# Quantisation without GpSimd and a new division of labour in the routing stage of a two-layer attention kernel

## The chip, the cores and the metric

One Trainium2 chip, one core. The metric is the device time in microseconds (us) of one execution, the median of several.

## The reference

What is computed, with B, S, D = 8, 512, 256, 16 heads and 8 experts:

```python
x = x + tanh(g_xattn[0]) * L0_xattn(layernorm(x), ctx)       # softmax attention
x = x + tanh(g_ffn[0])   * L0_ffn(layernorm(x))              # 2 of 8 experts per token, then a layer norm
x = x + tanh(g_xattn[1]) * L1_xattn(layernorm(x), ctx)
x = x + tanh(g_ffn[1])   * L1_ffn(layernorm(x))

def fake_quant_fp8(t):                                       # in L1_ffn, for x and for weight
    scale = 448.0 / maximum(max(abs(t)), 1e-12)
    return (t * scale).astype(float8_e4m3fn).astype(float32) / scale
L1_ffn = einsum('bsd,od->bso', fake_quant_fp8(x), fake_quant_fp8(weight)) + bias
```

The maximum is over the whole tensor, so nothing of the last layer can be scaled before the last layer norm is done.

## The kernel before

The kernel runs as ten stages, one after the other (`build`): `setup`, `project`, attention 0, `route`, `place`, `experts`, `combine`, attention 1, `merge`, `quantise`. Each stage has a program for each engine; a stage begins on all engines once the one before it has ended on all. Within a stage the order on each engine is written out by hand, and semaphores tie the engines together. Activations stand in SBUF as 128 partitions x 4 tiles x 256 columns for each of the 8 batches (`S.X` the residual, `S.BIG` the work copy), so an operation on a batch is 128x1024.

`route` (L979) ends attention 0. For each batch b, the reciprocals of the softmax sums are spread over the rows with two matmuls for each half k (`spread`, L671 and L672, all into the one PSUM bank pD); ScalarE copies the half to SBUF (`take_spread`, L1043); GpSimd multiplies the batch with it (`scale`, L1082); TensorE makes the output product (L975); VectorE adds it to the residual (L1100), takes the statistics (L341, L345), GpSimd raises to -1/2 (`Norm.power`, L350 and L353), VectorE normalises (`Norm.apply`, L361), TensorE turns the batch (L957), ScalarE takes it out (L1049), TensorE makes the router's logits (L964), VectorE copies them (L1107), the last thing in its round. VectorE clears a tile of zeros first (L1093), from which SyncE stores 8 MB. The reciprocal of the two last batches (`division.invert(LATE)`, L650) and its rounding into two parts (`cut_high`, `cut_low`) come at the stage's start.

`merge` (L1832) is the same for attention 1, with spreading banks for both halves, the scaling already on VectorE (L1897) and the normalising on ScalarE (L1876) with a product and a shift that GpSimd makes (L1887, L1889). VectorE also takes each batch's greatest magnitude (L1911). The reciprocal of the last two batches (L650) stands in VectorE's third round, `cut_low` (L659) in the fourth.

`quantise` (L1931) takes the maximum over partitions with GpSimd's all-reduce (L1971); VectorE makes scale, its inverse and the bias row from it, one after the other (L2035 to L2049). Then per batch: ScalarE scales (v, L1986); VectorE masks the exponent (m, L1821); GpSimd makes m into a rounding constant (max, then multiply, L1825); VectorE adds and subtracts it (L2076, L2079), the result in bf16; TensorE turns it (L2014); ScalarE takes it out (L2000, one buffer); TensorE multiplies with the quantised weight, four tiles of two bf16 matmuls (L2024) and one f32 matmul of a row of ones with the bias row (L2025); VectorE scales and adds the residual (L2062); SyncE stores. On TensorE each batch is turned, then waits for ScalarE's copy, then multiplied.

## Time and profile before

| | |
|---|---|
| Median of 3 runs | 1856.8 us (1854.93 to 1860.06) |
| The profiled execution | 1859.13 us, span 1857.1 us |
| Busy: TensorE, VectorE, ScalarE, GpSimd | 85%, 69%, 52%, 38% of the span |
| `route` | 519.4 to 605.8 us |
| `merge` | 1704.2 to 1760.8 us |
| `quantise` | 1761.1 us to the end |

The span holds instructions from first to last; about 2 us of the execution lie around it. Busy shares are averages over stages with different limits: what a change in one stage is worth is read from that stage's own timeline. In timeline rows the first number is the start and the second the duration; "x2" merges two instructions, and the bracket at the end gives how long the engine had been idle and who released it.

### The profile page before, as it was taken

The numbers are of one execution on the slowest core, as the hardware profiler recorded it, in microseconds if no ns is written. First come the engines' busy times: TensorE is split into PE (matmuls) and PEld (weight loads), VectorE is DVE, ScalarE is ACT, GpSimd is POOL, SyncE is SP. The second block draws the span as 40 slices with busy tenths as digits, with TensorE's granted clock in tenths as the row PEclk, the third lists the DMA queues.
The fourth block names the chain that finished last, engine by engine and source line by source line (L and its number), as shares of the span: only waits on it lengthen the run. The fifth ranks groups of instructions, "written<-read, shape, count | busy, mean of one in ns | idle before, by whom it ended". The sixth has DMA issues, their size and how long they took to land. (4 is left out here: it accounts for less than half of the span.)

```text
span 1857.1 us, 30481 instructions
## 1 busy us (share of the span) xinstructions
PE 1581.8 (85%) x11963; PEld 1035.1 (56%) x11963; DVE 1289.3 (69%) x1990; ACT 958.1 (52%) x1291; POOL 708.4 (38%) x954
## 2 busy tenths in 40 slices
PE   4873999999978269999999999688479999998558
PEld 3761333333357259999999999445223333334423
DVE  3655999999764856655555553478489999996843
ACT  2550888888822033444444444245248888885321
POOL 1651555555232044533333333333124545540252
PEclk9995999999987579999999999899779999999855
DMA  6556455555351212122212211356554555541001
GB/s 205 199 215 109 107 120 124 118 125 122 75 234 59 68 57 81 47 87 92 91 48 90 89 46 41 112 210 225 135 87 120 122 124 116 127 120 39 0 27 64
DMA packets 116766, 198.71 MB, mean 107 GB/s; under 512 B 28480, under 2 KB 62080, under 8 KB 115600
## 3 DMA queue, kind: packets, MB, share of 16 engines
q1 hardware_dynamic: 82480, 110.20, 20.0%
q0 software_dynamic: 34144, 86.56, 18.3%
q8 instruction: 95, 1.56, 0.4%
q14 instruction: 47, 0.39, 0.1%
HBM read 117.77 MB, written 77.87 MB: 105 GB/s over the span
## 5 line engine op out<-in xcount | busy, mean ns | idle before, releaser
L902 DVE TENSOR_REDUCE a_nmax<-a_ring 128x2 f32<-128x1024 f32 x512 | 608.7, 1220 | 40.1 <-PE a_ring L814 39.6
L884 ACT ACTIVATE a_pexp<-a_ring 128x1024 f32<-128x1024 f32 x512 | 522.6, 1027 | 195.7 <-PE a_ring L824 195.7
L836 PE MATMUL a_pout<-a_pexp,values 128*17 128x256 f32 x4096 | 321.5, 387 | 0.7 <-ACT a_pexp L884 0.7
L814 PE MATMUL a_ring<-a_k,a_q 64*128 64x512 f32 x1024 | 243.5, 474 | 54.1 <-DMA a_q<-qs 43.8
L1523 ACT ACTIVATE e_full<-e_pH,b1T 128x256 f32<-128x256 f32 x320 | 133.8, 469 | 272.3 <-PE e_pH L1483 269.8
L824 PE MATMUL a_ring<-a_q,a_k 64*128 64x512 f32 x1024 | 258.8, 502 | 12.8 <-DMA a_q<-a_nT 9.3
L1552 DVE TENSOR_TENSOR e_hid_lo<-e_full,e_hid_hi 128x512 fp32r<-128x512 f32 x160 | 128.2, 805 | 159.5 <-ACT e_hid_hi L1531 158.8
L824 PEld LDWEIGHTS a_ring<-a_q,a_k 64*128 64x128 f32 x1024 | 96.6, 185 | 235.2 <-DVE a_nmax L902 134.1
L1502 PE MATMUL e_pY<-fc_w_hi,e_hid_hi 128*128 128x256 f32 x640 | 186.0, 291 | 9.7 <-DVE e_hid_lo L1552 9.7
L1483 PE MATMUL e_pH<-e_rowsT_hi,fc_w1T_hi 128*128 128x256 f32 x640 | 182.3, 285 | 1.5 <-DVE e_rowsT_lo L1398 1.5
L1483 PE MATMUL e_pH<-e_rowsT_lo,fc_w1T_hi 128*128 128x256 f32 x640 | 182.1, 285 | 0.0
L1483 PE MATMUL e_pH<-e_rowsT_hi,fc_w1T_lo 128*128 128x256 f32 x640 | 182.0, 284 | 0.0
L1502 PE MATMUL e_pY<-fc_w_hi,e_hid_lo 128*128 128x256 f32 x640 | 180.9, 283 | 0.0
L1502 PE MATMUL e_pY<-fc_w_lo,e_hid_hi 128*128 128x256 f32 x640 | 180.9, 283 | 0.0
L814 PEld LDWEIGHTS a_ring<-a_k,a_q 64*128 64x128 f32 x1024 | 99.8, 192 | 130.7 <-DMA a_q<-qs 45.1
L723 POOL DMA_DIRECT2D a_k<-key_centre x56 | 32.0, 572 | 334.7 <-PE a_ring L824 334.7
L836 PEld LDWEIGHTS a_pout<-a_pexp,values 128*17 128x17 f32 x4096 | 68.3, 95 | 129.5 <-issue 126.6
L1502 PEld LDWEIGHTS e_pY<-fc_w_hi,e_hid_hi 128*128 128x128 f32 x640 | 122.4, 191 | 12.9 <-DVE e_hid_lo L1552 12.3
L1483 PEld LDWEIGHTS e_pH<-e_rowsT_hi,fc_w1T_hi 128*128 128x128 f32 x640 | 123.9, 194 | 1.9 <-DVE e_rowsT_lo L1398 1.9
L1483 PEld LDWEIGHTS e_pH<-e_rowsT_lo,fc_w1T_hi 128*128 128x128 f32 x640 | 124.0, 194 | 0.0
L1483 PEld LDWEIGHTS e_pH<-e_rowsT_hi,fc_w1T_lo 128*128 128x128 f32 x640 | 123.9, 194 | 0.0
L1502 PEld LDWEIGHTS e_pY<-fc_w_lo,e_hid_hi 128*128 128x128 f32 x640 | 122.6, 192 | 0.0
(295 smaller groups left out, 2570.1 us busy)
## 6 DMA issues: line engine op xcount, KB each, us to landing
outs<-a_osb SPq DMA_DIRECT2D x64, 256.0 KB, 2.7
fc_raw<-in_L_ffn_fc_w SPq DMA_DIRECT2D x16, 1024.0 KB, 5.6
a_k<-ks POOLq DMA_DIRECT2D x112, 128.0 KB, 3.4
a_q<-qs POOLq DMA_DIRECT2D x112, 128.0 KB, 3.6
BIG<-outs SPq DMA_DIRECT2D x64, 128.0 KB
ytok<-r_zeros SPq DMA_DIRECT2D x8, 1024.0 KB, 10.2
c_yg<-ytok POOLq DMA_DIRECT2D x16, 512.0 KB, 7.7
a_k<-ks POOLq DMA_DIRECT2D x112, 64.0 KB, 3.5
```

What stands on the lines that cost most here:

```text
L723: e.dma_start(k[j][lo:hi, :, :].bitcast(F32), S.key_centre[l][:, at].rearrange("s (o t) -> s o t", o=1).broadcast_to([hi - lo, 2, SEQ])).t ...
L814: mm = e.matmul(max_bank(m)[:, hh, :], q[j][at, p, t * P:(t + 1) * P], k[j][at, p, :], start=True, stop=True)
L824: mm = e.matmul(score_bank(n * U + i)[:, hh, :], k[j][at, p, t * P:(t + 1) * P], q[j][at, p, :], start=True, stop=True)
L836: mm = e.matmul(pout[n % 2][32 * h:32 * h + VW, at], v[:, b * TPB + t, g * HG + h, :], pexp[t][:, h, at], start=(t == 0 and half == 0), st ...
L884: e.activation(pexp[t][:, 2 * p:2 * p + 2, :], score_bank(n * U + i)[:, :, :], ACT.Exp).then_inc(exped, 1)
L902: e.tensor_reduce(nmax[n % 2][:, :].rearrange("p (x y t) -> p x y t", x=2, y=2)[:, :, p, t], max_bank(m)[:, :, :], AX.X, ALU.max, negate=T ...
L1483: mm = e.matmul(pH[q][:, f % 2, :], w1T[x][pl][:, k, f * P:(f + 1) * P], rowsT[j][pr][:, k, :], start=(k == 0 and n_pass == 0), stop=(k == ...
L1502: mm = e.matmul(pY[:, t, :], hid[pl][:, f, t * P:(t + 1) * P], w2[x][pr][:, f, :], start=(f == 0 and n_pass == 0), stop=(f == KF - 1 and n ...
L1523: ins = e.activation(full[q % 2][:, f % 2, :], pH[q][:, f % 2, :], ACT.Silu, bias=S.b1T[:, ds(n * KF + f, 1)])
L1552: e.tensor_tensor(hid[LO][:, 2 * q:2 * q + 2, :], full[q % 2][:, :, :], hid[HI][:, 2 * q:2 * q + 2, :], ALU.subtract).then_inc(lo, 1)
```

## The change

In `quantise`, GpSimd does nothing per batch any more. The maxima of the partitions (128x1) are turned into a row on TensorE and reduced by VectorE; 448 over the maximum is computed on one element and widened to all partitions by a matmul with a row of ones. The rounding constant is made by ScalarE, as Relu(m*MAGIC - LEAST), and VectorE's two operations add LEAST back (now scalar_tensor_tensor with two tensors and a constant). The bias row becomes three bf16 rows, at partitions 0, 32 and 64 of a 96-row operand that GpSimd clears, and its matmul is bf16 with 96 rows of ones. v has three buffers in the place of two, the turned batch two in the place of one; the order on TensorE stays turn, wait, multiply.

In `route`, the spread half is multiplied straight out of PSUM by VectorE (no copy on ScalarE, no GpSimd multiply), and ScalarE normalises with GpSimd's shift. The clearing of the zeros moves to GpSimd. TensorE's orders around `output` shift by one place, and the reciprocal stands behind VectorE's first four scalings. In `merge` the last reciprocal moves in front of the first update, `cut_high` to ScalarE's start and `cut_low` behind the first statistics. The diff, cut:

```diff
--- before.py
+++ after.py
+    def power_and_shift(self, e, b):
+        j = b % 2
+        self.power(e, b, j)
+        e.wait_ge(self.powed, b + 1)
+        e.tensor_tensor(self.product[j][:, :], self.mv[j][:, :, 0], self.rstd[j][:, :], ALU.mult).then_inc(self.shifted, 1)
+        e.wait_ge(self.shifted, 2 * b + 1)
+        e.tensor_scalar(self.shift[j][:, :], self.product[j][:, :], -1.0, None, ALU.mult).then_inc(self.shifted, 1)
+
+    def activate(self, e, b, src, dst):
+        j = b % 2
+        e.wait_ge(self.shifted, 2 * b + 2)
+        for t in range(TPB):
+            e.activation(dst[:, t, :], src[:, t, :], ACT.Identity, bias=self.shift[j][:, t:t + 1],
+                         scale=self.rstd[j][:, t:t + 1]).then_inc(self.normed, 1)
...
+    def scale(self, e, src, b, k):
+        rows = self.S.BIG[:, b * TPB + k * KD:b * TPB + (k + 1) * KD, :].rearrange("p t d -> p (t d)")
+        e.wait_ge(self.spread, b * KD + k + 1)
+        e.tensor_tensor(rows, rows, src[:, :], ALU.mult).then_inc(self.scaled, 1)
...
-                        e.wait_ge(division.copied, b * KD + k)
+                        e.wait_ge(division.scaled, b * KD + k)
                     division.spread_rows(e, pD, b, k)
 
                 def output(b):
-                    e.wait_ge(division.scaled, b + 1)
+                    e.wait_ge(division.scaled, (b + 1) * KD)
...
                 output(0)
                 spread(2, 0)
+                output(1)
                 spread(2, 1)
-                output(1)
                 for b in range(B):
                     if b + 3 < B:
                         spread(b + 3, 0)
                     turn_normed(b)
+                    if b + 2 < B:
+                        output(b + 2)
                     if b + 3 < B:
                         spread(b + 3, 1)
-                    if b + 2 < B:
-                        output(b + 2)
                     logits(b)
...
-                def take_spread(b, k):
-                    e.wait_ge(division.spread, b * KD + k + 1)
-                    if b >= 2:
-                        e.wait_ge(division.scaled, b - 1)
-                    e.activation(wide[b % 2][:, k, :], pD[:, :], ACT.Copy).then_inc(division.copied, 1)
...
+                for b in range(-1, B):
+                    if b >= 0:
+                        take_turned(b)
+                    if b + 1 < B:
+                        nb.activate(e, b + 1, S.X[:, tiles(b + 1), :], S.BIG[:, tiles(b + 1), :])
...
-                def scale(b):
-                    e.wait_ge(division.copied, (b + 1) * KD)
-                    rows = S.BIG[:, tiles(b), :].rearrange("p (k t) d -> p k (t d)", k=KD)
-                    e.tensor_tensor(rows, rows, wide[b % 2][:, :, :], ALU.mult).then_inc(division.scaled, 1)
-                scale(0)
-                scale(1)
+                e.memset(zeros[:, :, :], 0.0).then_inc(zeroed, 1)
                 for b in range(B):
-                    nb.power(e, b, b % 2)
-                    if b + 2 < B:
-                        scale(b + 2)
+                    nb.power_and_shift(e, b)
...
-                e.memset(zeros[:, :, :], 0.0).then_inc(zeroed, 1)
+                for b in range(2):
+                    for k in range(KD):
+                        division.scale(e, pD, b, k)
                 division.invert(e, LATE)
-                division.cut_low(e, LATE)
                 for i in range(B + 2):
                     if i < B:
                         x = S.X[:, tiles(i), :]
                         e.wait_ge(yd, i + 1)
                         e.scalar_tensor_tensor(out=x, in0=pY[i % 2][:, :, :], scalar=S.tg[:, 0:1], in1=x,
                                                op0=ALU.mult, op1=ALU.add).then_inc(upd, 1)
+                        if i and i + 1 < B:
+                            division.scale(e, pD, i + 1, 1)
                         e.wait_ge(upd, i + 1)
+                        if i >= 2:
+                            e.wait_ge(nb.shifted, 2 * i - 2)
+                            nb.wait(e, i - 2)
                         nb.stats(e, i, i % 2, x)
-                        nb.apply(e, i, i % 2, x, S.BIG[:, tiles(i), :])
+                        if i == 0:
+                            division.cut_low(e, LATE)
+                        if i + 2 < B:
+                            division.scale(e, pD, i + 2, 0)
...
+                division.cut_high(e, LATE)
+                    nb.activate(e, b, S.X[:, tiles(b), :], S.BIG[:, tiles(b), :])
...
+                division.invert(e, LATE)
                 for b in range(B + 1):
                     if b < B:
                         update(b)
-                        if b == 2:
-                            division.invert(e, LATE)
-                        if b == 3:
+                        if b == 0:
                             division.cut_low(e, LATE)
...
+MAGIC = 1.5 * 2.0 ** 20
+LEAST = 2.0 ** -6 * MAGIC
...
-                e.partition_all_reduce(amg[:, :], am[:, :], P, bass.bass_isa.ReduceOp.max).then_inc(red, 1)
-                @loop(e, B // 2)
-                def _(i):
-                    for j in range(2):
-                        if past(i * ROUNDED + MASKED):
-                            e.wait_ge(sc[j], i * ROUNDED + MASKED)
-                        make_m(e, m[j][:, :, :], m[j][:, :, :]).then_inc(sc[j], 1)
+                e.memset(ones[:, :], 1.0).then_inc(oned, 1)
+                e.memset(floor[:, :], -LEAST).then_inc(oned, 1)
+                e.memset(lifts[:, :], 0.0).then_inc(oned, 1)
...
+                def scale_rows(b):
+                    if b >= 3:
+                        e.wait_ge(added, b - 2)
+                    e.activation(v[b % 3][:, :, :], S.BIG[:, tiles(b), :], ACT.Copy, scale=scale[:, 0:1]).then_inc(scaled, 1)
+
+                def make(b):
+                    e.wait_ge(masked, b + 1)
+                    e.activation(m[b % 2][:, :, :], m[b % 2][:, :, :], ACT.Relu, bias=floor[:, 0:1], scale=MAGIC).then_inc(made, 1)
+
+                def take_turned(b):
+                    e.wait_ge(trv, b + 1)
+                    if b >= 2:
+                        e.wait_ge(yd, b - 1)
+                    e.activation(vqT[b % 2][:, :, :], pV[:, :, :], ACT.Copy).then_inc(vte, 1)
+
+                e.wait_ge(oned, 3)
+                e.wait_ge(scaled_by, 1)
+                scale_rows(0)
+                scale_rows(1)
+                make(0)
+                for b in range(B):
+                    if b + 2 < B:
+                        scale_rows(b + 2)
+                    if b + 1 < B:
+                        make(b + 1)
+                    take_turned(b)
...
-                                e.matmul(pY[j][:, t, :], vqT[:, k, t * P:(t + 1) * P], wqT[:, k, :], start=(k == 0), stop=False)
-                            last = e.matmul(pY[j][:, t, :], ones[:, :], lift[:, :], start=False, stop=True)
+                def turn_rounded(b):
+                    e.wait_ge(rounded, b + 1)
+                    if b:
+                        e.wait_ge(vte, b)
+                    for k in range(KD):
+                        for t in range(TPB):
+                            last = e.transpose(pV[:, k, t * P:(t + 1) * P], vq[b % 2][:, t, k * P:(k + 1) * P], S.identb[:, :])
+                    last.then_inc(trv, 1)
+
+                def output(b):
+                    e.wait_ge(vte, b + 1)
+                    if b >= 2:
+                        e.wait_ge(fin, b - 1)
+                    for t in range(TPB):
                         for k in range(KD):
-                            for t in range(TPB):
-                                last = e.transpose(pV[:, k, t * P:(t + 1) * P], vq[j][:, t, k * P:(k + 1) * P], S.identb[:, :])
-                        last.then_inc(trv, 1)
-                        if past(b + 1):
-                            e.wait_ge(vte, b + 1)
-                        if b >= 2:
-                            e.wait_ge(fin, b - 1)
-                        if b == 0:
-                            e.wait_ge(lifted, 3)
-                        for t in range(TPB):
-                            for k in range(KD):
-                                e.matmul(pY[j][:, t, :], vqT[:, k, t * P:(t + 1) * P], wqT[:, k, :], start=(k == 0), stop=False)
-                            last = e.matmul(pY[j][:, t, :], ones[:, :], lift[:, :], start=False, stop=True)
-                        last.then_inc(yd, 1)
+                            e.matmul(pY[b % 2][:, t, :], vqT[b % 2][:, k, t * P:(t + 1) * P], wqT[:, k, :], start=(k == 0), stop=False)
+                        last = e.matmul(pY[b % 2][:, t, :], S.onesb[0:rows, :], lifts[:, :], start=False, stop=True)
+                    last.then_inc(yd, 1)
+
+                e.wait_ge(most, 1)
+                e.transpose(pA[:, :], am[:, :], S.ident[:, :]).then_inc(turned, 1)
+                e.wait_ge(oned, 3)
+                e.wait_ge(factored, 4)
+                e.matmul(pB[:, :], ones[:, :], factor[:, :], start=True, stop=True).then_inc(widened, 1)
+                turn_rounded(0)
+                e.wait_ge(lifted, 8)
+                for b in range(B):
+                    output(b)
+                    if b + 1 < B:
+                        turn_rounded(b + 1)
...
+                def round_off(b):
+                    j = b % 2
+                    e.wait_ge(made, b + 1)
+                    if b >= 2:
+                        e.wait_ge(rounded, b - 1)
+                    e.scalar_tensor_tensor(out=big[j][:, :, :], in0=m[j][:, :, :], scalar=LEAST, in1=v[b % 3][:, :, :],
+                                           op0=ALU.add, op1=ALU.add).then_inc(added, 1)
+                    e.wait_ge(added, b + 1)
+                    if b >= 2:
+                        e.wait_ge(trv, b - 1)
+                    e.scalar_tensor_tensor(out=vq[j][:, :, :], in0=big[j][:, :, :], scalar=LEAST, in1=m[j][:, :, :],
+                                           op0=ALU.subtract, op1=ALU.subtract).then_inc(rounded, 1)
...
+                e.tensor_reduce(am[:, :], S.amax[:, :], AX.X, ALU.max).then_inc(most, 1)
+                e.wait_ge(turned, 1)
+                e.tensor_reduce(top[:, :], pA[:, :], AX.X, ALU.max).then_inc(factored, 1)
+                e.wait_ge(factored, 1)
+                e.tensor_scalar(kept[:, :], top[:, :], 1e-12, None, ALU.max).then_inc(factored, 1)
+                e.wait_ge(factored, 2)
+                e.reciprocal(rec[:, :], kept[:, :]).then_inc(factored, 1)
+                e.wait_ge(factored, 3)
+                e.tensor_scalar(factor[:, :], rec[:, :], FP8_MAX, None, ALU.mult).then_inc(factored, 1)
+                e.wait_ge(widened, 1)
+                e.tensor_copy(scale[:, :], pB[:, :]).then_inc(scaled_by, 1)
+                e.wait_ge(scaled_by, 1)
+                e.reciprocal(rscale[:, :], scale[:, :]).then_inc(inverse, 1)
+                e.tensor_scalar(lift[:, :], S.w["fb_b"][0:rows, :], S.wscale[0:rows, 0:1], scale[0:rows, 0:1], ALU.mult, ALU.mult).then_inc(lifted, 1)
+                e.wait_ge(inverse, 1)
+                e.tensor_tensor(inv1[:, :], rscale[:, :], S.wrscale[:, :], ALU.mult).then_inc(inverse, 1)
+                e.wait_ge(inverse, 2)
+                e.tensor_tensor(inv[:, :], inv1[:, :], S.tg[:, 3:4], ALU.mult).then_inc(inverse, 1)
+                mask(0)
+                e.wait_ge(oned, 3)
+                e.wait_ge(lifted, 1)
+                e.tensor_copy(lift1[:, :], lift[:, :]).then_inc(lifted, 1)
+                mask(1)
                 e.wait_ge(lifted, 2)
-                e.tensor_scalar(lift[:, :], lift[:, :], scale[0:1, 0:1], None, ALU.mult).then_inc(lifted, 1)
-                def exponents(b, i, j):
-                    if past(b + 1):
-                        e.wait_ge(vs, b + 1)
-                    if past(i * ROUNDED):
-                        e.wait_ge(sc[j], i * ROUNDED)
-                    mask_exponent(e, m[j][:, :, :], v[j][:, :, :]).then_inc(sc[j], 1)
-                def output(b, i, j):
-                    e.wait_ge(yd, b + 1)
-                    if past(16 * i):
-                        e.wait_ge(st[j], 16 * i)
-                    e.scalar_tensor_tensor(out=o[j][:, :, :], in0=pY[j][:, :, :], scalar=inv[:, 0:1], in1=S.X[:, tiles(b), :],
-                                           op0=ALU.mult, op1=ALU.add).then_inc(fin, 1)
-                exponents(0, 0, 0)
-                @rounds(e, 1, 1)
-                def _(b, j, i):
-                    if inside(b + 1):
-                        exponents(b + 1, i + j, 1 - j)
-                    if inside(b):
-                        if past(i * ROUNDED + MADE):
-                            e.wait_ge(sc[j], i * ROUNDED + MADE)
-                        if past(b):
-                            e.wait_ge(trv, b)
-                        e.tensor_tensor(big[j][:, :, :], v[j][:, :, :], m[j][:, :, :], ALU.add).then_inc(sc[j], 1)
-                        if past(i * ROUNDED + ADDED):
-                            e.wait_ge(sc[j], i * ROUNDED + ADDED)
-                        e.tensor_tensor(vq[j][:, :, :], big[j][:, :, :], m[j][:, :, :], ALU.subtract).then_inc(sc[j], 1)
-                    if inside(b - 1):
-                        output(b - 1, i + j - 1, 1 - j)
+                e.tensor_tensor(rest1[:, :], lift[:, :], lift1[:, :], ALU.subtract).then_inc(lifted, 1)
+                e.tensor_copy(lifts[0:1, :], lift1[0:1, :]).then_inc(lifted, 1)
+                e.wait_ge(lifted, 4)
+                e.tensor_copy(lift2[:, :], rest1[:, :]).then_inc(lifted, 1)
+                e.wait_ge(lifted, 5)
+                e.tensor_tensor(rest2[:, :], rest1[:, :], lift2[:, :], ALU.subtract).then_inc(lifted, 1)
+                e.tensor_copy(lifts[32:33, :], lift2[32:33, :]).then_inc(lifted, 1)
+                e.wait_ge(lifted, 7)
+                e.tensor_copy(lifts[64:65, :], rest2[64:65, :]).then_inc(lifted, 1)
+                e.wait_ge(inverse, 3)
+                for b in range(B + 1):
+                    if b and b + 1 < B:
+                        mask(b + 1)
+                    if b < B:
+                        round_off(b)
+                    if b:
+                        output(b - 1)
```

## Rows read from the trace of the kernel before

**Rows 1.** Table by stretch: route, quantise (busy us PE, PEld, DVE, ACT, POOL; clock).

```profile
519.30:606.00 86.70, 72.69 (x352) 62.14 (x352) 51.51 (x115) 17.83 (x25) 28.87 (x24) 0.80 0.39 148
...
1761.00:1857.10 96.10, 62.29 (x192) 26.26 (x192) 41.14 (x42) 17.27 (x16) 36.23 (x9) 0.50 0.13 44
```

**Rows 2.** Timeline of one steady batch in quantise: start us, duration us, engine.

```profile
1790.04 1.03 PE L2014 MATMUL q_pV<-identb,q_vq 128*128 128x128 bf16 x8
...
1791.11 1.02 ACT L2000 ACTIVATE q_vqT<-q_pV 128x1024 bf16<-128x1024 bf16 x1 [5.89 <-PE q_pV L2014]
...
1792.19 0.61 PE L2024 MATMUL q_pY<-wk,q_vqT 128*128 128x256 bf16 x2 [1.12 <-ACT q_vqT L2000]
...
1792.73 1.21 PE L2025 MATMUL q_pY<-q_lift,q_ones 1*128 1x256 f32 x2
...
1798.93 1.03 PE L2014 MATMUL q_pV<-identb,q_vq 128*128 128x128 bf16 x8
```

**Rows 3.** Tiles (ns min/median/max) and groups by line (busy us, mean ns).

```profile
L2079 DVE TENSOR_TENSOR q_vq<-q_big,q_m x8: 1224/1940/1941, 1779.1 to 1837.1; 128x1024 bf16<-128x1024 f32 x8
...
L1821 DVE TENSOR_SCALAR q_m<-q_v x8: 682/684/695, 1769.7 to 1826.9; 128x1024 int32<-128x1024 int32 x8
...
L1679 DVE SCALAR_TENSOR_TENSOR BIG<-c_yg,gate,BIG 128x256 f32<-128x256 f32 x64 | 26.7, 478 | 15.3 <-DMA c_yg<-ytok 15.0
...
L884 ACT ACT_TABLE_LOAD x1 | 1.3, 1283 | 10.0 <-PEq L1630 10.0
```

**Rows 4.** Timeline, head and last output of quantise.

```profile
1761.09 0.16 DVE L2031 TENSOR_REDUCE q_am<-amax 128x1 f32<-128x8 f32 x1 [0.33 <-PEq L1843]
...
1766.94 0.38 POOL L1971 PARTITION_ALL_REDUCE q_amg<-q_am  x1 [9.54 <-issue]
...
1768.51 2.19 ACT L1986 ACTIVATE q_v<-BIG,q_scale 128x1024 f32<-128x1024 f32 x2 [9.00 <-DVE q_inv L2045]
...
1781.14 1.03 PE L2014 MATMUL q_pV<-identb,q_vq 128*128 128x128 bf16 x8 [30.31 <-DVE q_vq L2079]
...
1852.40 1.28 DVE L2062 SCALAR_TENSOR_TENSOR q_o<-q_pY,q_inv,X 128x1024 f32<-128x1024 f32 x1 [7.61 <-PE q_pY L2025]
```

**Rows 5.** Timeline of merge, around the reciprocal and at its end.

```profile
1712.61 1.28 DVE L1902 SCALAR_TENSOR_TENSOR X<-m_pY,tg,X 128x1024 f32<-128x1024 f32 x1 [3.39 <-PE m_pY L975]
...
1725.50 3.35 DVE L650 RECIPROCAL d_rec<-d_den 32x512 f32<-32x512 f32 x1
...
1729.62 0.50 PE L671 MATMUL m_pD<-d_parts,d_pick 96*128 96x512 f32 x1 [3.94 <-DVE BIG L1897]
...
1755.46 0.23 POOL L350 TENSOR_SCALAR m_var<-m_mv 128x4 f32<-128x4 f32 x1 [2.20 <-DVE m_mv L345]
...
1759.54 1.22 DVE L1911 TENSOR_REDUCE amax<-BIG 128x1 f32<-128x1024 f32 x1 [2.93 <-ACT BIG L1876]
```

**Rows 6.** Groups by line: spreading's takers, and a GpSimd memset.

```profile
L1897 DVE TENSOR_TENSOR BIG<-BIG,m_pD 128x512 f32<-128x512 f32 x16 | 10.3, 676 | 6.7 <-PE m_pD L672 6.6
...
L1043 ACT ACTIVATE r_wide<-r_pD 128x512 f32<-128x512 f32 x16 | 9.5, 595 | 43.1 <-PE r_pD L672 43.1
...
L790 POOL MEMSET a_k<- 128x1024 f32 x8 | 7.2, 952 | 30.2 <-POOLq L1630 20.8 <-POOLq L468 9.4
```

**Rows 7.** Timeline of route: reciprocal, first update, TensorE round, stalled one, end.

```profile
522.72 3.35 DVE L650 RECIPROCAL d_rec<-d_den 32x512 f32<-32x512 f32 x1 [1.25 <-DMA d_den<-outs]
...
531.00 1.28 DVE L1100 SCALAR_TENSOR_TENSOR X<-r_pY,tg,X 128x1024 f32<-128x1024 f32 x1 [1.08 <-PE r_pY L975]
...
545.44 1.85 PE L964 MATMUL r_pL<-wg,r_hT 128*128 128x8 f32 x16
...
549.12 3.62 PE L975 MATMUL r_pY<-wo,BIG 128*128 128x256 f32 x16
...
555.13 2.84 PE L964 MATMUL r_pL<-wg,r_hT 128*128 128x8 f32 x16 [2.40 <-DVE logit L1107]
...
605.56 0.19 DVE L1107 COPY logit<-r_pL 128x32 f32<-128x32 f32 x1 [6.30 <-PE r_pL L964]
```

136 lines of the change are left out of this document (40 added, 96 removed).

## The prediction

> **What bounds the kernel now.** I read the table by stretch first. TensorE is 85% busy over the whole span, but the change touches three stages at the edges of the long ones, and there other things decide. In `quantise` (96.1 us) the granted clock is 0.50, so TensorE runs at 1.2 GHz, and no engine but TensorE passes half of the time; in `route` (86.7 us) TensorE is busy for 72.7 us at a mean clock of 0.80 [rows 1].
>
> Then the timeline of one steady batch in `quantise` [rows 2]. Turning starts at 1790.04, ScalarE takes the result out at 1791.11, the first product starts at 1792.19 and the next turning at 1798.93. The period is 8.89 us: 2.15 from turning to product (turn 1.03, copy 1.02, two hand-overs of about 0.05) and 6.74 of products, that is 4 x 1.685. Within one of the four, the two bf16 matmuls take 0.54 (1792.19 to 1792.73) and the f32 bias matmul the other 1.145. The reader should see that VectorE and GpSimd set nothing here: the bias of one row costs more than the data. GpSimd does two harms elsewhere: in the head its all-reduce and its first constant lie on the path (below), and VectorE's subtraction takes 1.94 us in the median against 1.22 at the least, in the last batch, which had no GpSimd pass beside it [rows 3].
>
> The head: maximum of each partition at 1761.09, all-reduce at 1766.94, scaling at 1768.51, first turning at 1781.14. The tail: last output at 1852.40, then 4.7 us to the span's end [rows 4].
>
> In `merge` VectorE bounds, and its 3.35 us reciprocal at 1725.50 makes TensorE wait 3.94 us, while at 1712.61 VectorE had been idle for 3.39 us [rows 5]. In `route` the first update is at 531.00 and the last copy ends at 605.75; a round of logits, spread, turn, spread takes 3.68 us (545.44 to 549.12), the product after it 3.42 of issue (3.62 less the 0.2 of the last one's way through); in other rounds TensorE waits up to 2.40 us for VectorE's copy of the logits, and what follows runs slower (logits 2.84 in the place of 1.85) [rows 7].
>
> **Quantise, steady part.** Removed: four f32 one-row matmuls per batch, the GpSimd pass. Added: four bf16 matmuls with 96 rows, one ScalarE pass. No row shows a 96-row bf16 matmul of 256 columns; the nearest is the L2024 pair, 0.54 for two with the change to f32 behind it, and 0.61 less a last way of 0.4, so 0.21, from one to the next [rows 2]. Bounds for a tile of three: 3 x 0.21 = 0.64, and 0.54 + 0.27 = 0.81; a gain beyond 0.64 needs a faster clock, a rival below. I take 0.64, because the eight turnings follow each other without gaps though each loads weights too. Products: 4 x 0.64 = 2.56, period 2.15 + 2.56 = 4.71, gain 4.18 per batch, 33.4 for eight. With 0.81 the period is 5.39 and the gain 28.0.
>
> What comes late next is VectorE, as each batch needs mask 0.69, two three-operand passes and the output 1.28. The nearest row for the passes over SBUF is L1679, 0.48 for 256 columns, 4 in some 1.7; for 1,024 at once the least of the subtraction, 1.22, and the output's 1.28 bracket them [rows 3, 4]. Sum 0.69 + 1.28 + 1.22 + 1.28 = 4.47, less some 0.07 of overlap between independent neighbours, twice: 4.33, under 4.71 by 0.38. ScalarE: 1.10 (2.19 for two), a second such pass for the constant, 1.02: 3.2 [rows 2, 4]. Its order puts the constant ahead of the copy, but the mask it waits for ends some 2.5 us earlier, so nothing queues. The third v lets it run ahead. The second turned buffer buys nothing, as the order is unchanged. Output stores of 0.5 MB have two buffers, and the last takes with everything 4.7 less 1.28 = 3.4, under 2 x 4.71.
>
> One rule speaks against moving the constant. Rows: ScalarE's pass costs 1.10, VectorE's masking pass of the same size 0.69 [rows 3, 4]. The Trainium skill, page ScalarE: Activation LUTs, section Rules for kernel authors, says that relu, max and mul belong on VectorE. By it VectorE would need 4.33 + 0.61 = 4.94, and the period would be that; here the slower engine is the better one, by 0.2 us per batch.
>
> **Quantise, head.** Before, from the maxima's end (1761.25) to scaling (1768.51) 7.26 us. Now a one-column f32 transpose, five VectorE steps of about 0.19 (like the 0.16 of q_am with its hand-over), one f32 matmul. The two TensorE steps have no row; below, 0.31 each (a turning of 1.03 less seven starts of 0.1), above, 1.21 each (the f32 pair) [rows 2, 4]. I take 0.75 and 0.55, nearer to the small ones, plus hand-overs: 2.5 us, range 1.8 to 3.8. Scaling starts at 1763.75. Then scaling 1.15, mask, second scaling, second mask to 1766.7; the bias parts, seven small passes of which six come after it, between 0.16 and 0.48 each, I take 1.75 in all: 1768.45. They are on the path, as the first constant is there by 1767.2. Add and subtract, 2.55: first turning at 1771.05 in the place of 1781.14, gain 10.1, range 8.5 to 11.5. The tail stays. GpSimd's three small memsets end long before use.
>
> **Merge.** The reciprocal moves into VectorE's idle 3.39 us: cover 3.39, need 3.35 [rows 5]. Nothing else is before the first update, and the sums that it reads are there: it has to begin at 1712.6 - 3.35 = 1709.3, 5.1 us after the stage's start, and in `route`, where it waits for the same load, it began 3.3 us after the start (522.72 [rows 7]). `cut_low` only changes rounds. VectorE is busy throughout afterwards, so all 3.35 is gained less a hand-over: 3.3. Without that cover it would be 0.
>
> **Route.** Start: four scalings of 0.68 follow each other through one bank where copies of 0.60 did [rows 6], and the fourth is not ahead of the product: first update 531.5, 0.5 later. The clearing of zeros on GpSimd (twice the size of the 0.95 us memset [rows 6], so 1.9) stays beside this; GpSimd's first other work waits for the first statistics, after 531.5. Update 1 follows a spread and a product later, at 535.8; TensorE's first round waits for it and one scaling behind it: 537.8. From there TensorE runs five rounds of 3.68 + 3.42 = 7.10 [rows 7]: VectorE has update 1.28, scaling 2 x 0.68, statistics 1.8, copy 0.2, 4.6 in all, and its copy of the logits no longer stands behind the normalising. The tightest link is product, update, scaling, next spread: 0.2 + 1.28 + 0.68 + 0.1 = 2.26 beside spread and logits, 2.2. So 35.5 + 0.3 for the first round's wait gives 573.6, turn and last product 578.1. The tail: update 1.28, statistics 1.8, then GpSimd and ScalarE 4.08 (1755.46 to 1759.54 in `merge` [rows 5]), turning at the low clock 2.0, copy 1.0, logits 3.6, copy 0.2: 14.1 with hand-overs, 592.2. Gain 605.75 - 592.2 = 13.5. At full clock the tail is 2.6 shorter; if waits in the early rounds bring the low clock back as in the 2.84 row, the gain is 6 to 8.
>
> **Sum.** 33.4 + 10.1 + 3.3 + 13.5 = 60.3. Against the profiled execution (1859.1, span 1857.1) that gives 1798.8. The median of the runs, 1856.8, is 2.3 lower, so 1796.5; I forecast 1797.
>
> **Rivals.** (A) TensorE reaches its high level (2.4 GHz) in `quantise`. For: the new products fill 96 or 128 rows. Against: it was 87% busy (1.12 idle of 8.89) at the low level [rows 1, 2], and will be less busy now. Then VectorE's 4.33 bounds: 8 x 0.38 less again, 1794. The Trainium skill, page TensorE: Matmul & The Clock Gate, section What's actually happening, says that the throttled state is the default and activity releases it; its Part 4 that transposes don't count as activity. By the first this rival is likelier than the row suggests; the trace agrees that turnings alone do not raise it.
> (B) `route` gives half: the link of 2.26 slips, and the clock falls after each wait. For: the stage's mean clock was 0.80 [rows 1]. Gain 6 to 8: 1803.
> (C) The bias matmul pays a slot of its own whatever its type: half of the 1.145 stays, the tile takes 0.54 + 0.57 = 1.11, the period 6.6, 15 us more: 1812.
> (D) The change from Copy to Relu and back loads a table each time, 1.28 us [rows 3]: ScalarE 3.2 + 2.6 = 5.8 per batch, 1.1 x 8 = 9 more: 1806. Against: Exp and Copy alternate in attention under one load.
> (E) Slower than before, by (D) at a larger price: from a period of 8.89 + (10.1 + 3.3 + 13.5)/8 = 12.3 all gains are gone, that is when one load costs over (12.3 - 3.2)/2 = 4.5 us. The load's row has 10.0 idle us before it; if that were its price, the period is 3.2 + 2 x 11.3 = 25.8 and the time 1797 + 8 x 21.1 = 1966. Against: the idle time there is a stage's start.
> (F) The change doesn't do what it says: TensorE waits for VectorE, as the two passes cost 1.94 even without GpSimd beside them. Period 4.33 + 1.38 = 5.7, 8 more: 1805.
>
> **How the numbers follow.** Forecast 0.50 (1797); A 0.16; B 0.13; C 0.08; D 0.03; F 0.05; E 0.01; the rest, gains lost in ways I don't see, 0.04. Low end: A with the warm tail and the short head, 1794 - 2.6 - 1.4, some 1789. High end: B with the dearer tiles of 0.81 (5.4), 1809, and part of C: 1812. A difference under 0.3% could not be told from none. Faster by more than that 0.97, within 0.01, slower 0.02.
>
> **What would show it.** Right: in `quantise` turnings 4.7 us apart, VectorE close to 4.3 busy of them, no GpSimd pass, clock 0.50; scaling about 2.5 us after the maxima; reciprocal in `merge` ended before the first update; rounds of 7.1 in `route` and its end near 592. Wrong: turnings over 5.4 apart (C, F, by what TensorE was released by), rounds over 8 in `route` (B), table loads between activations (D).

## The result and the profile after

The changed kernel takes 1795.7 us (median of four runs, 1792.5 to 1798.9); the kernel before, beside it on the same chip, 1858.4 (1854.9 to 1864.1). The ratio is 0.966, with an interval of 0.9626 to 0.9693. The profiled execution took 1793.3 us with a span of 1791.5, where that of before took 1859.1 with 1857.1.

The table by stretch, after (columns as in [rows 1]: busy us of PE, PEld, DVE, ACT, POOL with instruction counts, granted clock, DMA share, GB/s). The first line is `route`, then two stretches of it, then `quantise`, then three stretches of that.

```profile
521.10:596.40 75.30, 67.61 (x352) 58.20 (x352) 38.74 (x98) 25.31 (x41) 15.80 (x34) 0.84 0.44 170
555.00:560.00 5.00, 5.00 (x34) 4.58 (x34) 3.43 (x12) 1.15 (x2) 1.71 (x4) 1.00 0.31 105
540.00:545.00 5.00, 4.30 (x17) 3.69 (x17) 1.66 (x8) 2.94 (x6) 1.72 (x4) 0.66 0.98 383
1741.60:1791.50 49.90, 25.75 (x163) 18.45 (x163) 37.73 (x49) 25.01 (x24) 0.47 (x3) 0.64 0.25 85
1756.00:1761.00 5.00, 3.88 (x24) 2.76 (x23) 4.24 (x4) 3.10 (x3) 0.00 (x0) 0.50 0.31 105
1766.00:1771.00 5.00, 2.90 (x26) 2.18 (x24) 4.97 (x5) 3.10 (x3) 0.00 (x0) 0.84 0.32 107
1781.00:1788.00 7.00, 3.62 (x32) 2.62 (x32) 4.83 (x5) 1.42 (x2) 0.00 (x0) 1.00 0.46 152
```

What the reader should see: `quantise` fell from 96.0 to 49.9 us and `route` from 86.7 to 75.3. In `quantise` GpSimd is down from 36.23 us to 0.47 (three memsets), and VectorE, busy for 37.7 of 49.9 us, is now the busiest engine. The clock is at its low level (0.50, 1.2 GHz) in most batches, as before, but not in all: 0.84 in one stretch in the middle, 1.00 in the last two batches.

The timeline of a steady batch after, against [rows 2] (start us, duration us, engine, and in brackets the idle time before it):

```profile
1756.11 1.06 PE L2013 MATMUL q_pV<-identb,q_vq 128*128 128x128 bf16 x8
...
1757.20 1.02 ACT L1991 ACTIVATE q_vqT<-q_pV 128x1024 bf16<-128x1024 bf16 x1 [1.68 <-PE q_pV L2013]
...
1758.28 0.61 PE L2022 MATMUL q_pY<-wk,q_vqT 128*128 128x256 bf16 x2 [1.12 <-ACT q_vqT L1991]
...
1758.69 0.42 PE L2023 MATMUL q_pY<-q_lifts,onesb 96*128 96x256 bf16 x1
...
1758.90 0.64 PE L2022 MATMUL q_pY<-wk,q_vqT 128*128 128x256 bf16 x2
...
1760.82 1.06 PE L2013 MATMUL q_pV<-identb,q_vq 128*128 128x128 bf16 x8
...
1761.07 1.28 DVE L2063 SCALAR_TENSOR_TENSOR q_o<-q_pY,q_inv,X 128x1024 f32<-128x1024 f32 x1 [0.44 <-PE q_pY L2023]
```

From turning to turning it is 4.71 us where it was 8.89: 2.17 up to the first product as before, then four tiles of 0.64 (1758.28 to 1758.90 and so on) where there were four of 1.685. VectorE waits only 0.44 us of the period for TensorE.

Where the time went, by stage (us; a stage runs from its first instruction, GpSimd's memsets left out, to the next one's):

| stretch | before | after | gain | forecast |
|---|---|---|---|---|
| `route` | 86.7 | 75.3 | 11.4 | 13.5 |
| `merge` | 56.9 | 53.9 | 3.0 | 3.3 |
| `quantise` | 96.0 | 49.9 | 46.1 | 43.5 |
| everything else | 1617.5 | 1612.4 | 5.1 | 0 |

The three edited stages give 60.5 us. The last row is scatter only in part. The matmuls of the expert stage, which no edit touches, take 506.0 to 507.2 us from the first to the last in the three kernels with the old `route` (the one before, and `q_only` and `m_only` below) and 502.3 to 504.7 in the eleven with the new one. The two ranges don't meet, so some 3 us go with the new `route`; how, no run here shows. Combine with the attention behind it takes 524.9 to 532.2 us, with no such order.

### The profile page after: what moved, and what is told of

Read it like the earlier page. It is cut to its first block and busy times, and to the rows that moved or that the text cites. A ratio compares the mean times of both kernels' runs of the same rounds, so it can differ in the third digit from the quotient of the medians.

```text
span 1791.5 us, 30430 instructions
## 1 busy us (share of the span) xinstructions
PE 1532.7 (86%) x11934; PEld 1019.2 (57%) x11934; DVE 1272.4 (71%) x1980; ACT 970.8 (54%) x1315; POOL 661.0 (37%) x957
```

## The experiments

**One part at a time.** Three kernels, each the one before with one stage of the change in it. `q_only` has the new `quantise` alone:

```diff
+                    e.activation(m[b % 2][:, :, :], m[b % 2][:, :, :], ACT.Relu, bias=floor[:, 0:1], scale=MAGIC).then_inc(made, 1)
...
-                            last = e.matmul(pY[j][:, t, :], ones[:, :], lift[:, :], start=False, stop=True)
...
+                        last = e.matmul(pY[b % 2][:, t, :], S.onesb[0:rows, :], lifts[:, :], start=False, stop=True)
...
```

> The kernel before with the quantise stage of the changed one, nothing else. If the stages' gains add up, as the sum of the prediction has it: the quantise stage ends 46 us sooner after its first maximum (49.9 us in the place of 96.0, as in the changed kernel's trace), route and merge stay at 86.7 and 56.9 us, and the time is about 1858.4 - 46 = 1812. Rival: the experts and attention stages, which stand between the edited ones and came out 5 us shorter in the one profiled execution of the changed kernel, follow from an edit (addresses, order of semaphores); then some of the 5 us shows here or in one of the next two.

`r_only` has the new `route` alone (scaling on VectorE from the bank, normalising on ScalarE):

```diff
+                        nb.activate(e, b + 1, S.X[:, tiles(b + 1), :], S.BIG[:, tiles(b + 1), :])
...
-                        nb.apply(e, i, i % 2, x, S.BIG[:, tiles(i), :])
...
+                        if i + 2 < B:
+                            division.scale(e, pD, i + 2, 0)
```

> The kernel before with the changed route stage alone. Adding up: route 75.3 us in the place of 86.7, time about 1858.4 - 11.4 = 1847. Rival: what comes behind route (placing, experts) gives part of it back, or gains a further 4 us: time 1843 or under, or 1850 or over.

`m_only` has the moved reciprocal of `merge` alone:

```diff
+                division.invert(e, LATE)
...
-                        if b == 2:
-                            division.invert(e, LATE)
-                        if b == 3:
+                        if b == 0:
```

> The kernel before with the reciprocal of the last two batches moved ahead of the first update in merge, and the two steps behind it. Adding up: merge 53.9 us in the place of 56.9, time about 1855.5. Rival: the reciprocal waits for its load or delays the first update, merge 55.5 us or more.

Measured, against 1861.8 for the kernel before on that chip: `q_only` 1815.5 (ratio 0.9765, interval 0.9743 to 0.9786), its `quantise` 49.3 us; `r_only` 1847.1 (0.9932, 0.9911 to 0.9953), its `route` 75.0; `m_only` 1857.5 over ten runs (0.9983, 0.9973 to 0.9992), its `merge` 53.3. The product of the three ratios is 0.968, and that of the whole change is 0.966 with an interval that holds it. What follows: the parts add up, each stage's own gain is about the same with and without the others, and `merge` gives about 3.5 us that show in the whole time only as 0.2%. `r_only` gained 14.7 us where its stage gave 11.7; its interval (9 to 17) is too wide to tell the expert stage's part from none, and its expert matmuls, 504.7 us, lie nearest to the old range.

**What bound quantise.** `bias_f32` keeps everything of the change but the type and rows of the bias matmul:

```diff
-                        last = e.matmul(pY[b % 2][:, t, :], S.onesb[0:rows, :], lifts[:, :], start=False, stop=True)
+                        last = e.matmul(pY[b % 2][:, t, :], ones[:, :], lift[0:1, :], start=False, stop=True)
```

> The changed kernel with one edit undone: the bias goes into the products as one f32 row with a row of ones again, in the place of the three bf16 rows. If the period of quantise was set by TensorE's f32 matmuls: turnings 8.9 us apart again, 4.2 x 8 = 33 us more, time about 1795.7 + 33 = 1829. Rival: the gain came from GpSimd's leaving (VectorE's subtraction back from 1.94 to 1.22 us, no hand-over to GpSimd), and the matmul's type only fills idle time of TensorE: turnings stay under 6 us apart, time under 1805.

It took 1834.8 us (0.9862, 0.9839 to 0.9886) and its `quantise` 85.8. Two turnings and the output between them, then the waits of that stage, by sum, count and longest:

```profile
1765.74 1.03 PE L2013 MATMUL q_pV<-identb,q_vq 128*128 128x128 bf16 x8
1765.85 1.28 DVE L2063 SCALAR_TENSOR_TENSOR q_o<-q_pY,q_inv,X 128x1024 f32<-128x1024 f32 x1 [5.93 <-PE q_pY L2023]
...
1774.64 1.03 PE L2013 MATMUL q_pV<-identb,q_vq 128*128 128x128 bf16 x8
```

```profile
ACT q_vqT L1991 <- PE q_pV L2013: 46.8, 8, 7.9
DVE q_o L2063 <- PE q_pY L2023: 41.9, 8, 7.6
```

The period is 8.90 again, although GpSimd does nothing there and VectorE's passes take 1.22 us each: VectorE waits 41.9 us for the products. So the f32 bias of one row was the bound, and neither GpSimd nor its effect on VectorE was. Whether its type or its single row costs the time is open: no run has a one-row bf16 bias or a 96-row f32 one. What the rest of the change brings without it is the head: `bias_f32` is 10.2 us shorter than before in this stage.

**Where the constant is made.** Two kernels move it off ScalarE. `const_gpsimd` gives it back to GpSimd, with the two-operand passes of before:

```diff
+                for b in range(B):
+                    e.wait_ge(masked, b + 1)
+                    make_m(e, m[b % 2][:, :, :], m[b % 2][:, :, :]).then_inc(made, 1)
...
-                    e.activation(m[b % 2][:, :, :], m[b % 2][:, :, :], ACT.Relu, bias=floor[:, 0:1], scale=MAGIC).then_inc(made, 1)
...
+                    e.tensor_tensor(big[j][:, :, :], v[b % 3][:, :, :], m[j][:, :, :], ALU.add).then_inc(added, 1)
...
+                    e.tensor_tensor(vq[j][:, :, :], big[j][:, :, :], m[j][:, :, :], ALU.subtract).then_inc(rounded, 1)
```

> The changed kernel with the rounding constant made by GpSimd again (max, then multiply, 4.5 us a batch) and VectorE's two passes as before; the head, the bias and the stages ahead stay changed. If TensorE's chain and the bias matmul carried the gain: GpSimd's pass runs beside it and costs VectorE its second passes' 1.94 us, so the period goes from 4.7 to 5.1 to 5.5, 3 to 6 us more, and the head is 2.5 us longer: time about 1802. Rival: GpSimd's leaving is what gave the gain; then the period goes towards 8.9 and the time over 1815.

`const_vector` does the same with `make_m` on VectorE, ahead of the addition:

```diff
-                    e.activation(m[b % 2][:, :, :], m[b % 2][:, :, :], ACT.Relu, bias=floor[:, 0:1], scale=MAGIC).then_inc(made, 1)
...
+                    e.wait_ge(masked, b + 1)
+                    make_m(e, m[j][:, :, :], m[j][:, :, :]).then_inc(made, 1)
```

> The changed kernel with the rounding constant made by VectorE (one masking-like pass of 0.69 us more), as the Trainium skill, page ScalarE: Activation LUTs, section Rules for kernel authors, would have it for relu, max and mul. By the sum VectorE then needs 4.94 to 5.0 us a batch, more than TensorE's chain of 4.71: period 5.0, about 2 us more. Rival: the chain has the room, period stays 4.7 and the time within 0.5 us; or VectorE's pass without its own hand-over makes it shorter.

Against 1860.7 for before they took 1797.8 (0.9666, 0.9642 to 0.9691) and 1799.9 (0.9665, 0.9639 to 0.969): by the whole time neither differs from the change. The stage tells them apart: 55.1 and 53.4 us against 49.9. One period of `const_gpsimd`, 5.16 us, on VectorE, GpSimd and TensorE:

```profile
1767.59 1.27 DVE L2057 SCALAR_TENSOR_TENSOR q_o<-q_pY,q_inv,X 128x1024 f32<-128x1024 f32 x1
...
1767.72 1.04 PE L2009 MATMUL q_pV<-identb,q_vq 128*128 128x128 bf16 x8 [0.99 <-DVE q_vq L2051]
1768.78 0.94 DVE L1834 TENSOR_SCALAR q_m<-q_v 128x1024 int32<-128x1024 int32 x1
1769.64 1.21 DVE L2047 TENSOR_TENSOR q_big<-q_v,q_m 128x1024 f32<-128x1024 f32 x1
1769.80 4.53 POOL L1838 TENSOR_SCALAR q_m<-q_m 128x1024 f32<-128x1024 f32 x1 [0.63 <-DVE q_m L1834]
1770.88 1.94 DVE L2051 TENSOR_TENSOR q_vq<-q_big,q_m 128x1024 bf16<-128x1024 f32 x1
```

VectorE has no idle time in it: 0.94, 1.21, 1.94 and 1.27 follow each other, and TensorE waits for `vq`. The subtraction's 1.94 and the mask's 0.94 (0.68 without GpSimd) make VectorE the bound once the bias is cheap. GpSimd's leaving is therefore worth about 5 us, as `const_gpsimd` loses 5.2 of the 46.1: 2.2 in the head (11.9 against 9.7 us from the maxima's reduction to the first turning) and the rest in the batches.

In `const_vector` the constant's pass takes 0.68 us and the period is 4.91 to 4.92 in three of seven batches. The Trainium skill (ScalarE: Activation LUTs, Rules for kernel authors) would have relu, max and mul on VectorE. Pass for pass the trace agrees (0.68 against ScalarE's 1.13), but VectorE was the fuller engine, and the stage got 3.5 us longer.

How far can a stage's length be trusted? The changed `quantise`, word for word the same, took 49.3, 49.9, 50.6 and 50.6 us in the profiled executions of `q_only`, the change, `product_first` and `norm_vector`; its head was 9.7 in each, and its periods differed with the granted clock. Differences of about 1 us in this stage mean little by themselves; heads and single periods at a known clock mean more.

**The head.** `late_lifts` moves the seven small passes that make the bias parts (six of them behind the second mask) from ahead of the first addition to behind the first subtraction:

```diff
                 mask(0)
-                e.wait_ge(oned, 3)
-                e.wait_ge(lifted, 1)
-                e.tensor_copy(lift1[:, :], lift[:, :]).then_inc(lifted, 1)
...
                         round_off(b)
+                    if b == 0:
+                        lift_parts()
```

> The changed kernel with VectorE's seven small passes for the bias rows moved behind its first rounded batch. If they lie on the path in the head and have cover behind it: first turning 1.7 to 2.0 us sooner after the maxima (7.9 in the place of 9.8), second period up by at most 0.4, time 1.5 us less. Rival: they only change places, the second turning comes as late as before, nothing gained.

Three executions took 1792.9 to 1799.0 us, the median 1793.4 (0.9651, 0.9617 to 0.9685); a fourth, of 7558 us, is left out. The head is 8.3 us for 9.7, so 1.4 shorter where 1.7 to 2.0 was expected, the first period 5.25 for 4.75, the stage 48.9 for 49.9. The passes are on the path at either place; behind the subtraction 0.5 of the 1.4 us comes back, as the next rounding waits for them.

**TensorE a batch ahead.** `ahead` uses the second turned buffer: TensorE turns batch b + 1 before it multiplies batch b, and VectorE puts its output one batch later:

```diff
                 for b in range(B):
+                    if b + 2 < B:
+                        turn_rounded(b + 1)
                     output(b)
-                    if b + 1 < B:
+                    if b + 2 == B:
                         turn_rounded(b + 1)
...
-                    if b:
-                        output(b - 1)
+                    if b >= 2:
+                        output(b - 2)
```

> The changed kernel with TensorE turning the next batch ahead of the product of this one, so that ScalarE's copy runs beside the product, and VectorE's output step one batch later. If the 4.71 us are turn, copy, product in a row: TensorE then needs only 3.4, and VectorE's own 4.33 bounds: period 4.3 to 4.4, 2 to 3 us less. Rival: VectorE waits elsewhere already (4.7 or more stays), or the added batch of delay is paid at the end and eats the gain: within 0.5 us.

It took 1794.1 us (0.9647, 0.9623 to 0.967), the stage 45.7. Its table by stretch over ten us in the middle (columns as above):

```profile
1760.00:1770.00 10.00, 4.97 (x46) 3.82 (x47) 9.93 (x10) 6.79 (x7) 0.00 (x0) 0.83 0.36 122
```

VectorE is busy for 9.93 of 10.00 us and the period is 4.19. That is VectorE's own floor, made of starts: mask 0.60, addition 1.26, subtraction 1.14, output 1.19. The copy between turning and product is hidden now, and in the steady batches nothing but VectorE is left. It stays so where the granted clock falls: the periods from 1765.22 and 1769.41 are 4.19 too, at 0.65 and 0.53. The last output meets another limit, the store that has to free its buffer:

```profile
1781.41 1.28 DVE L2065 SCALAR_TENSOR_TENSOR q_o<-q_pY,q_inv,X 128x1024 f32<-128x1024 f32 x1 [1.83 <-DMA out_x<-q_o]
```

It is 4.2 us less in the stage; by the whole time it can't be told from the change.

`ahead_late` is `ahead` with the passes of `late_lifts` moved as well:

```diff
+                    if b + 2 < B:
+                        turn_rounded(b + 1)
...
+                    if b == 0:
+                        lift_parts()
+                    if b >= 2:
+                        output(b - 2)
```

> The changed kernel with both edits that helped its quantise stage: TensorE turns the next batch ahead of the product (period 4.19, VectorE's own, 4.2 us less in that stage) and the small passes for the bias stand behind the first rounded batch (1.0 us less). If both are on one chain, one after the other, the gains add up: quantise 44.7 us in the place of 49.9, time about 1790.5. Rival: with VectorE as the bound every pass of it counts wherever it stands, so that moving the small passes gains nothing any more: quantise 45.7.

It took 1796.1 us over five runs (0.9671, 0.9656 to 0.9686) and its stage 47.0: a head of 8.3, then periods of 5.29, 3.37, 4.57, three of 4.19 and 4.93. The two gains don't add, and the stage is longer than either expected value (44.7 or 45.7). Where VectorE is the bound, small passes on it count wherever they stand, and here they leave idle time behind as well:

```profile
1751.23 1.23 DVE L2053 SCALAR_TENSOR_TENSOR q_big<-q_m,q_v 128x1024 f32<-128x1024 f32 x1 [0.42 <-ACT q_m L1985]
...
1762.68 1.28 DVE L2065 SCALAR_TENSOR_TENSOR q_o<-q_pY,q_inv,X 128x1024 f32<-128x1024 f32 x1 [0.52 <-PE q_pY L2023]
```

In the head VectorE now waits 0.35 us ahead of the second mask and 0.42 ahead of the first addition, both for ScalarE, where the small passes had filled the time; so the head is 1.4 us shorter, but the passes take 2.2 behind the subtraction, and the first output then waits 0.52 for TensorE. The pair is 1.3 us longer than `ahead` alone in the stage, no more than equal code differs by; the rows show no gain from it.

**The clock.** `kept_at_work` gives TensorE five bf16 matmuls of 256 columns after each turning, into a bank that nobody reads, in the time in which it would wait for ScalarE's copy:

```diff
                 def output(b):
+                    for n in range(5):
+                        e.matmul(pZ[:, 0:D], S.onesb[:, :], wqT[:, 0, :], start=True, stop=True)
                     e.wait_ge(vte, b + 1)
```

> The changed kernel with five more bf16 matmuls of 256 columns for each batch in quantise (into a bank that nobody reads), where TensorE waits for ScalarE's copy; results are unchanged. If TensorE's clock in this stage is at the low level because it rests too much: it rises to the high level and stays, TensorE's chain falls under VectorE's 4.2 (which the trace of the run with turning ahead shows), period 4.2, about 3 us less. Rival: the clock stays at 0.50 as with the one-row f32 matmuls, and the five, 1.07 us in a wait of 1.12, leave the period at 4.7 or add up to 0.3 each, 0 to 2 us more.

It took 1792.7 us (0.9642, 0.9616 to 0.9668), the stage 47.2. Its table by stretch:

```profile
1756.00:1761.00 5.00, 3.12 (x30) 2.14 (x28) 4.97 (x6) 3.55 (x4) 0.00 (x0) 1.00 0.31 105
1761.00:1766.00 5.00, 4.25 (x26) 2.87 (x25) 4.82 (x7) 3.50 (x4) 0.00 (x0) 0.66 0.31 107
1766.00:1771.00 5.00, 3.44 (x32) 2.63 (x33) 4.97 (x6) 4.08 (x5) 0.00 (x0) 1.00 0.39 134
1771.00:1776.00 5.00, 3.40 (x32) 2.34 (x30) 4.93 (x6) 3.42 (x4) 0.00 (x0) 1.00 0.49 161
```

The clock is at its high level in most stretches, and three of the seven periods are 4.19, VectorE's floor again (4.97 of 5.00 busy). Three others take 4.42 to 4.53: each holds or follows a product at the low level. From the first turning on, the mean granted clock was 0.89, against 0.64 to 0.71 in the four executions of the changed `quantise` without the added matmuls. This shows rival A's mechanism: at 2.4 GHz the products don't bound and VectorE does. It is worth 2.7 us in the stage, less than a run's scatter. The Trainium skill (TensorE: Matmul & The Clock Gate, What's actually happening) says that throttled is the default and activity releases it; the added matmuls raised the clock, which agrees.

**The routing stage.** `product_first` puts the product of batch 2 ahead of the first turning, for which TensorE waits in the change:

```diff
+                    if b == 0:
+                        output(b + 2)
                     turn_normed(b)
-                    if b + 2 < B:
+                    if b and b + 2 < B:
                         output(b + 2)
```

> The changed kernel with the product of batch 2 put ahead of the turning of batch 0 in route. In the changed kernel TensorE waits 1.14 us for the first normalised batch, and turning and product behind it run at the low clock (1.97 and 4.45 us). If that wait is what cost the 2 us of route that the prediction gave too much: it goes, and what follows stays at the high clock: route 2 to 3 us shorter, 72.5 to 73.5. Rival: the clock falls for another reason (the single spreads before it), or the round only waits later: within 0.5 us of 75.3.

It took 1795.5 us (0.9647, 0.9619 to 0.9674) and its `route` 75.6, nothing gained. The change's own timeline there, then that of `product_first`:

```profile
537.66 0.50 PE L695 MATMUL r_pD<-d_parts,d_pick 96*128 96x512 f32 x1 [0.75 <-DVE BIG L683]
...
539.45 0.50 PE L695 MATMUL r_pD<-d_parts,d_pick 96*128 96x512 f32 x1 [1.05 <-DVE BIG L683]
...
540.88 1.97 PE L981 MATMUL r_pH<-ident,BIG 128*128 128x128 f32 x8 [0.70 <-ACT BIG L380]
...
542.64 4.45 PE L999 MATMUL r_pY<-wo,BIG 128*128 128x256 f32 x16
...
547.40 1.85 PE L988 MATMUL r_pL<-wg,r_hT 128*128 128x8 f32 x16
...
554.46 1.85 PE L988 MATMUL r_pL<-wg,r_hT 128*128 128x8 f32 x16
```

```profile
539.27 3.62 PE L999 MATMUL r_pY<-wo,BIG 128*128 128x256 f32 x16
542.72 1.04 PE L981 MATMUL r_pH<-ident,BIG 128*128 128x128 f32 x8
...
544.87 1.95 PE L988 MATMUL r_pL<-wg,r_hT 128*128 128x8 f32 x16 [0.65 <-ACT r_hT L1069]
...
547.24 1.85 PE L981 MATMUL r_pH<-ident,BIG 128*128 128x128 f32 x8
548.88 4.52 PE L999 MATMUL r_pY<-wo,BIG 128*128 128x256 f32 x16
```

In the change TensorE waits three times before its first turning (0.75, 1.05, 0.70); that turning then takes 1.97 us for 1.04 and the product 4.45 for 3.62. In `product_first` the wait of 0.70 is gone and turning and product run at the high level (1.04, 3.62), but with the product gone from between them the logits wait 0.65 for ScalarE's copy, and the low level comes one turning later (1.85 and 4.52). The slow stretch followed the short waits and was only moved. That these short waits cause it is the reading that fits both traces; no run here removed all of them, so it is not shown.

`norm_vector` puts the normalising of `route` back on VectorE and leaves the scaling there too:

```diff
-                    if b + 1 < B:
-                        nb.activate(e, b + 1, S.X[:, tiles(b + 1), :], S.BIG[:, tiles(b + 1), :])
...
                         nb.stats(e, i, i % 2, x)
+                        nb.apply(e, i, i % 2, x, S.BIG[:, tiles(i), :])
```

> The changed kernel with the normalising in route on VectorE again (as before), the scaling still on VectorE out of PSUM. If TensorE's rounds of 7.1 us bound the stage: VectorE has 4.6 + 1.4 us a round (without GpSimd beside it the four passes take 1.38, not 3.35) and still fits, ScalarE's 2.08 and GpSimd's shift are off the last chain, so route stays at 75 us or is 1 us shorter. Rival: VectorE's copy of the logits again stands behind the normalising, TensorE waits for it and falls to the low clock: rounds of 8 and more, route 80 us or more.

It took 1804.0 us (0.9696, 0.9672 to 0.9721) and its `route` 81.6, so 6.3 longer. Its table by stretch, then two waits of its timeline:

```profile
550.00:590.00 40.00, 39.57 (x249) 34.91 (x247) 30.28 (x86) 5.12 (x5) 8.54 (x20) 1.00 0.22 74
590.00:600.00 10.00, 5.59 (x27) 5.09 (x25) 1.93 (x10) 2.05 (x2) 1.71 (x4) 0.51 0.16 52
```

```profile
541.97 0.50 PE L695 MATMUL r_pD<-d_parts,d_pick 96*128 96x512 f32 x1 [3.68 <-DVE BIG L683]
...
593.42 3.55 PE L988 MATMUL r_pL<-wg,r_hT 128*128 128x8 f32 x16 [3.30 <-DVE logit L1118]
```

The rounds are not where it loses most: from 550 to 590 us TensorE is busy for 39.57 of 40.00 us at full clock, with the normalising on VectorE; a round takes 7.28 us for 7.05, which is 1 us in all. Most of the loss is at both ends, about 3 us in the opening and 2 at the end. In the opening the spread waits 3.68 us for a scaling that stands behind the first normalising, and at the end the logits wait 3.30 for VectorE's copy that stands behind the last normalising; they then run at the low level. So the size that was set against my view came out, but not by rounds of 8 us: it comes mostly from two places in the order of VectorE's work.

## Why the prediction was right, and where it only came out right

The forecast was 1797 and the range 1789 to 1812; 1795.7 was measured. Step by step:

- **The bias matmul.** Four tiles of 0.64 and 2.15 before them, 4.71: measured 4.71 in three periods of seven. The value was taken as the lower of two bounds (0.64 and 0.81), and the lower was right: the 96-row matmul costs what one of the 128-row ones costs. Rival C is out by this, and `bias_f32` shows that this one instruction carries 35.9 of the stage's 46.1 us (85.8 against 49.9).
- **VectorE late next.** The two passes from SBUF cost 1.22 each beside nothing, as bracketed, so F is out. The sum of 4.33 was 0.14 too large: the floor measured in `ahead` and `kept_at_work` is 4.19. Both passes cost 1.22 where I had put 1.28 for one of them, and there are three overlaps of 0.08 or 0.09, less one gap of 0.04, where I had two overlaps of 0.07: the passes behind the mask, behind the subtraction and behind the output all begin before these have ended. With the constant on VectorE I had 4.94; `const_vector` has 4.92.
- **The head.** Scaling at 2.5 us after the maxima's end: measured 2.28 (1741.79 to 1744.07). The head's lines:

```profile
1741.85 0.37 PE L2027 MATMUL q_pA<-ident,q_am 128*1 128x128 f32 x1 [10.48 <-DVE q_am L2066]
1742.26 0.28 DVE L2068 TENSOR_REDUCE q_top<-q_pA 1x1 f32<-1x128 f32 x1 [0.46 <-PE q_pA L2027]
...
1743.22 0.55 PE L2030 MATMUL q_pB<-q_factor,q_ones 1*128 1x1 f32 x2 [1.00 <-DVE q_factor L2074]
...
1744.07 2.19 ACT L1981 ACTIVATE q_v<-BIG,q_scale 128x1024 f32<-128x1024 f32 x2 [4.01 <-DVE q_scale L2076]
...
1748.82 1.22 DVE L2051 SCALAR_TENSOR_TENSOR q_big<-q_m,q_v 128x1024 f32<-128x1024 f32 x1
...
1751.36 1.04 PE L2013 MATMUL q_pV<-identb,q_vq 128*128 128x128 bf16 x8 [7.58 <-DVE q_vq L2056]
```

  Of the two steps on TensorE, which had no row, the second was met (0.55), the first was set at 0.75 and is 0.37. The six small passes are on the path, as said: the addition starts at 1748.82, 4.75 us after the scaling, where I had 4.7. The gain is 10.3 for 10.1.
- **The tail and the clock.** "The tail stays" was wrong by 1.5 us: from the last turning to the span's end it is 8.0 us for 13.7, and only 4.2 of these 5.7 were in the sum. The reason is the clock of the last two batches (1.00), which also made the last period 3.97. The tail's 1.5, some 0.9 over the seven periods (4.58 and 3.97 among them) and 0.2 of the head are the 2.6 us by which `quantise` beat the forecast. Rival A, put at 0.16 as a state of the whole stage, came true for some batches only, and this differs between executions: `norm_vector`, whose `quantise` is the same code, has three periods of 4.18 to 4.19. One sentence under rival A, that the trace agrees that turnings alone do not raise the clock, had no row behind it: the turnings of `quantise` never run without products between them.
- **Merge.** The step holds: the reciprocal has ended before the first update is released, which then has to wait only for TensorE.

```profile
1692.72 3.35 DVE L669 RECIPROCAL d_rec<-d_den 32x512 f32<-32x512 f32 x1
...
1696.83 1.28 DVE L1903 SCALAR_TENSOR_TENSOR X<-m_pY,tg,X 128x1024 f32<-128x1024 f32 x1 [0.76 <-PE m_pY L999]
```

  The 3.39 us idle of [rows 5] are filled and 0.76 is left; the gain is 3.0 in this execution and 3.3 to 3.8 in the others (`merge` takes 53.2 to 53.9 us in the eleven kernels with the new order, 56.8 to 57.3 in the three without it).
- **Route.** The opening came as worked out: the first update 11.9 us after the stage's start (531.5 less 519.3 is 12.2), the first round's spread 18.3 after it (18.5). The rounds are 7.05 us at full clock (547.40, 554.46), for 7.10. The tail from the last product's end to the end of the last copy is 14.3 for 14.1. The missing 2.1 us are in one term: "0.3 for the first round's wait". The first round took 9.66 us (539.45 to 549.11) where the sum had 7.4. It was a wait for the first normalised batch as well, and what stood behind it ran at the low level, 0.93 more for the turning and 0.83 for the product. I had named this as what would make the gain 6 to 8 (rival B), had it come back in several rounds; it came once.
- **Table loads** (D, E): no load stands between Copy and Relu anywhere in `quantise`; ScalarE's scaling, constant and copy follow each other without one.

So the mechanism held in every step but two, the tail that was to stay and the size of the first round's wait in `route`, both by the clock's level. The sum of 60.3 against the 60.5 measured in the edited stages owes its closeness to these errors of opposite sign, 2.6 too little in `quantise` and 2.1 too much in `route`; that part is luck. The profiled execution lay another 5 us lower, in stages that the change does not touch: the forecast had nothing there, and some 3 us of it, in the expert stage, came with the new `route` every time. That earns the forecast nothing either.

No version beats the change by more than a measurement tells. `ahead` and `kept_at_work` are ahead by 4.2 and 2.7 us in the stage, and their ratios are low (0.9647, 0.9642), but `product_first`, which gained nothing in its stage, has 0.9647 as well, and all three intervals hold 0.966.

## What to carry to other kernels

Read one period of a loop from start to start on the engine that never waits long, and price each instruction in it, small ones too: here a one-row f32 bias cost twice as much as the data, while the engine that looked slow (GpSimd) bound nothing in the period, though its all-reduce and first constant did in the head. Once the bound is gone, sum the next engine's period at once; it was 0.5 us behind, so further work on TensorE was worth some 4 us, and which engine takes a pass is decided by that sum, not by which does it faster. A total that comes out right can hide errors of opposite sign: compare stage by stage.
